# Two layers of graph convolution: layer one by relation ahead of the gathers, its messages summed by static ranges of destinations, layer two all dense

## The reference

```python
edge_index = jnp.stack([src, dst])
h = jnp.maximum(_layernorm(x, axis=-1), 0.0)
# layer one: x + _L0(h)
h_all = jnp.einsum('ni,roi->rno', node_repr, weight)
msgs = h_all[edge_types, src]
messages = jax.ops.segment_sum(msgs, dst, num_segments=node_repr.shape[0])
# + bias
h = jnp.maximum(_layernorm(x, axis=-1), 0.0)
# layer two: x + _L1(h)
h = x @ W
src, dst = edges and one loop per node; deg = segment_sum(1, dst)
norm = dinv[src] * dinv[dst]
out = segment_sum(norm[:, None] * h[src], dst) + b
return jax.nn.leaky_relu(out, negative_slope=0.2)
```

## Time and profile before

| | |
|---|---|
| median of three runs | 2851.63 us (2846.8 to 2854.67) |
| profiled execution, span | 2849.6 us |
| mean granted clock of TensorE | 0.928 |
| PE matmul busy | 2338.5 us, 82% |
| PE weight load busy | 1739.1 us, 61% |
| DVE busy | 1215.3 us, 43% |
| ACT busy | 1320.0 us, 46% |
| GpSimd (POOL) busy | 1693.0 us, 59% |
| moved by DMA | 464.38 MB, mean 163 GB/s |

### The profile page before, as it was taken

How to read it: one execution, slowest core, us unless ns; L and a number is a source line. 1 busy time by engine, 2 the same in 40 slices (tenths; PEclk the granted TensorE clock), 3 DMA queues, 4 the chain that set the end, 5 groups by cost and what they waited for, 6 DMA issues and landing times.

```text
span 2849.6 us, 45882 instructions
## 1 busy us (share of the span) xinstructions
PE 2338.5 (82%) x15616; PEld 1739.1 (61%) x15616; DVE 1215.3 (43%) x3492; ACT 1320.0 (46%) x3283; POOL 1693.0 (59%) x1754
## 2 busy tenths in 40 slices
PE   2357677777887888888888999999999999989887
PEld 2356666666666666666666666666666666656345
DVE  8345556556556565555555222222222222222228
ACT  5336655565656566565666343434344343433000
POOL 4666666656656666666666666666666666662530
PEclk9578888888999999999999999999999999999999
DMA  8335446545555655656556455545454454543665
GB/s 278 90 100 154 146 156 183 159 148 170 187 173 178 193 170 185 189 175 201 174 168 205 146 160 157 160 145 167 137 157 146 138 155 143 156 134 86 200 177 170
DMA packets 325692, 464.38 MB, mean 163 GB/s; under 512 B 61414, under 2 KB 252822, under 8 KB 325462
## 3 DMA queue, kind: packets, MB, share of 16 engines
q0 software_dynamic: 83168, 228.90, 28.3%
q1 hardware_dynamic: 198198, 149.60, 17.5%
q10 hardware_dynamic: 44096, 82.95, 7.8%
HBM read 352.28 MB, written 109.01 MB: 162 GB/s over the span
## 4 chain that ended last, share of the span: by engine, by line
PE 70%; issue 11%; ACT 7%; DVE 4%; another core or an unknown queue 3%; ACTq 1%; DMA 1%; POOL 1%; DVEq 0%; POOLq 0%; SPq 0%
PE ps_slot L1556 24%; PE ps_slot L1630 15%; PE ps_proj L1587 13%; PE ps_aux L1630 11%; PE ps_slot L1601 6%; ACT staging_f L1202 2%; ACT gap_f L1257 2%; ACT onehot_f L1265 1%; ACT acc_f L1188 1%; DVE hots_f L1435 1%; DVE acc_f L1478 1%; DVE acc_f L1483 1%; DVE acc_f L1475 1%; DVE hots_f L1432 1%
## 5 line engine op out<-in xcount | busy, mean ns | idle before, releaser
L1058 POOL DMA_INDIRECT rows_f<-table,idxT x1617 | 1565.3, 968 | 904.8 <-issue 404.4
L1556 PE MATMUL ps_slot<-onehot_f,rows_f 128*128 128x128 f32 x6468 | 916.1, 295 | 138.7 <-issue 71.9
L1556 PEld LDWEIGHTS ps_slot<-onehot_f,rows_f 128*128 128x128 f32 x6468 | 864.4, 207 | 188.8 <-issue 125.7
L1257 ACT ACTIVATE gap_f<-iota,keyT 128x128 bf16<-128x128 bf16 x1617 | 529.4, 394 | 91.8 <-issue 44.8
L1202 ACT ACTIVATE staging_f<-ps_slot 128x400 bf16<-128x400 f32 x768 | 348.0, 500 | 479.7 <-remote 228.7
L1265 ACT ACTIVATE onehot_f<-gap_f 128x384 f32<-128x384 bf16 x539 | 278.4, 516 | 560.2 <-remote 349.0
L1630 PE MATMUL ps_slot<-abuf_f,stash_f 128*128 128x512 bf16 x1890 | 457.6, 387 | 51.0 <-issue 48.8
L1432 DVE TENSOR_TENSOR hots_f<-iota_m_f,key_e_f 128x400 bf16<-128x400 bf16 x768 | 279.1, 363 | 455.2 <-PE ps_slot L1601 234.3
L1630 PE MATMUL ps_aux<-abuf_f,stash_f 128*128 128x512 bf16 x1710 | 410.9, 390 | 20.4 <-issue 19.5
L1587 PE MATMUL ps_proj<-w0t,acc_f 128*128 128x256 f32 x1600 | 389.7, 394 | 20.0 <-issue 19.2
L1346 DVE TENSOR_TENSOR acc_f<-ps_slot,acc_f 128x256 f32 (+1 forms) x561 | 232.0, 414 | 404.6 <-remote 220.8
(11 more groups left out here) (159 smaller groups left out, 816.4 us busy)
## 6 DMA issues: line engine op xcount, KB each, us to landing
abuf_f<-counts_d SPq DMA_DIRECT2D x120, 640.0 KB
rows_f<-table,idxT POOLq DMA_INDIRECT x1683
stash_f<-table SPq DMA_DIRECT2D x20, 960.0 KB
table<-hs_f SPq DMA_DIRECT2D x50, 192.0 KB
table<-xres SPq DMA_DIRECT2D x10, 640.0 KB, 7.6
x_d<-x_f SPq DMA_DIRECT2D x50, 128.0 KB
acc_f<-x_d SPq DMA_DIRECT2D x50, 128.0 KB, 2.2
xt_f<-in_x_dram SPq DMA_DIRECT2D x48, 128.0 KB
```

The lines of the kernel that those rows point to most:

```text
L1058: eng.indirect_dma_start(rows0[:, k, c, :], None, V["table0"], bass.IndirectOffsetOnAxis(ap=idxT[:, n * LOT + c:n * LOT + c + 1], axis=0)) ...
L1257: last = eng.activation(gap[:, n % 2, c, :], iota[:, :], ACT.Abs, scale=-1.0, bias=V["key"][:, n * LOT + c:n * LOT + c + 1])
L1556: last = eng.matmul(o[:, b * W:(b + 1) * W], rows0[:, k, c, b * P:(b + 1) * P], onehot[:, n % HOTS, c, :], start=(c == 0), stop=(c == LOT ...
```

## The change

Layer one is turned round: the first block projects every tile of nodes with all eight matrices and stores the results, and the gathers fetch messages that are ready.

- `table0` has 50 x 128 x 8 rows, one for each node and relation, each in three bf16 pieces of 256 (high, middle and low part of the float32 number): 1536 bytes a row. The index of an edge is (source + 64) x 8 + type.
- In the first block PE takes each tile through two transposes (`turn`), DVE copies them (`copy_turned`), and PE projects in two halves of four relations (`project`, `k = 2t + h`), each into two banks of PSUM; the halves alternate between two such pairs. ACT casts a half to bf16 (`high`), DVE subtracts (`remainder`), ACT casts the rest (`middle`), GpSimd subtracts again (`low`), and SP stores the tile, of which `parts` holds two. The preparation of the edges is spread among the tiles by number.
- In the second block a slot is a quad of four chunks. DVE builds a one-hot of 128 destinations (destination modulo 128) for each chunk. Destinations fall into 98 windows of 128 that step by 64; which chunks belong to which window is fixed at build time, and the first block checks that it is so. PE sums a window's chunks in one PSUM bank (three bf16 matmuls of 256 columns a chunk), and DVE adds it to the rows of x, in two or three parts.
- The bias is added on its own in stage A. The float32 sums, `acc`, its clearing, the projection in tiles and the bias in three pieces are gone.
- Layer two counts 800 windows (all 50 tiles) over `COUNT_SLOTS = 320` slots. The gathers behind the loop are gone. There are 13 groups (the last of two tiles) and 10 batches, so 260 pieces. The plan's account has `PACE = 3.9` and 3.6 us a piece. Two banks serve the closes instead of four, and six the late dense pieces instead of four.

The path for edges that don't fit (`aggregate_any`) is changed as well; it does not run here.

```diff
-RING0 = 7
+RING = 6
-PACE = 3.85
+PACE = 3.9
+PIECE = 3.6
+COUNT_SLOTS = 320
-    table0 = nc.dram_tensor("table0", (T * P, DF), f32).ap()
+    table0 = nc.dram_tensor("table0", (T * P * R, DF3), bf16).ap()
 # SP, first block
+                for t in range(T):
+                    eng.wait_ge(S["lo"], 2 * (t + 1))
+                    eng.dma_start(table0[t * P * R:(t + 1) * P * R, :].rearrange("(p r) d -> p (r d)", p=P),
+                                  parts[:, t % 2, :, :].rearrange("p r d -> p (r d)")).then_inc(s_t0[t % 2], 16)
 # ACT, first block
+                def high(k):
+                    t, h = divmod(k, 2)
+                    eng.wait_ge(S["pj"], k + 1)
+                    if t >= 2 and h == 0:
+                        eng.wait_ge(s_t0[t % 2], 16 * (t // 2))
+                    eng.activation(parts[:, t % 2, h * R // 2:(h + 1) * R // 2, 0:DF],
+                                   pair_bank(k).rearrange("p b (r d) -> p (b r) d", d=DF), ACT.Copy).then_inc(S["hi"], 1)
+                for t in range(T):
+                    high(2 * t)
+                    if t > 0:
+                        middle(2 * t - 1)
+                    if t + 2 < T:
+                        normalize(t + 2)
+                    high(2 * t + 1)
+                    middle(2 * t)
 # GpSimd, first block
+                def low(k):
+                    t, h = divmod(k, 2)
+                    eng.wait_ge(S["mid"], k + 1)
+                    rows = parts[:, t % 2, h * R // 2:(h + 1) * R // 2, :]
+                    eng.tensor_tensor(rows[:, :, 2 * DF:DF3], r1[:, k % 2, :, :], rows[:, :, DF:2 * DF], ALU.subtract).then_inc(S["lo"], 1)
 # PE, first block
+                    for h in range(2):
+                        k = 2 * t + h
+                        if k >= 2:
+                            eng.wait_ge(S["r1"], k - 1)
+                        for j in range(2):
+                            r = h * R // 2 + 2 * j
+                            for b in range(NB):
+                                last = eng.matmul(pair_bank(k)[:, j, :].rearrange("p (r d) -> p r d", d=DF), ht[:, t % 2, b, :], w0t[:, r:r + 2, b, :],
+                                                  start=(b == 0), stop=(b == NB - 1))
 # GpSimd, second block
-                for c in range(LOT):
-                    eng.indirect_dma_start(rows0[:, k, c, :], None, V["table0"],
+                if n >= RING:
+                    eng.wait_ge(s_pe, n - RING + 1)
+                for c in range(QUAD):
+                    eng.indirect_dma_start(rows[:, k, c, :], None, V["table0"],
 # DVE, second block
+                eng.tensor_tensor(onehot[:, n % HOTS, :, :], iota4[:, :, :],
+                                  V["key"][:, n * QUAD:(n + 1) * QUAD].unsqueeze(1).to_broadcast([P, P, QUAD]), ALU.is_equal).then_inc(s_oh, 1)
+                    add_rows(u, P // 4, P // 2, s)
+                    add_rows(u, P // 2, P, s)
+                    add_rows(u + 1, 0, P // 4, s)
 # PE, second block
+                for c in range(QUAD):
+                    i = n * QUAD + c
+                    s = PL.window[i]
+                    if PL.opens[i] and s >= 2:
+                        eng.wait_ge(s_msg, windows_added(s - 1))
+                    for p in range(3):
+                        last = eng.matmul(window_part(s), onehot[:, n % HOTS, :, c], rows[:, k, c, p * DF:(p + 1) * DF],
+                                          start=(PL.opens[i] and p == 0), stop=(PL.closes[i] and p == 2))
 # Plan
-                pe += 1.3 + 0.28 * len(self.win.get(n - LEAD, ())) + (3.45 if n >= LOTS and n % LOTS in PROJECT_AT else 0.0)
-            limit = (n + 1) * PACE + (3.0 if n < self.nlot else 0.0)
+                pe += 1.45 + 0.31 * len(self.win.get(n - LEAD, ()))
+            limit = (n + 1) * PACE + 3.0
```

More of the change, by code:

```diff
@@ L335, in _ @@
             @block.vector
             def _(eng):
-                seg_f, base, rel, orig = (small[:, i, :] for i in range(4))
                 ne = [0]
@@ L494, in _ @@
-                if ahead(n - 5):
-                    eng.wait_ge(S["acp"], n - 5)
-                eng.transpose(ps_slot[0:KT, n % 6, 0:P], small[:, 2, :], ident[:, :]).then_inc(S["etp"], 1)
-                n += 1
-                eng.wait_ge(S["below"], (KC + 1) // 2)
-                eng.wait_ge(S["below_odd"], KC // 2)
-                for b in range(D.looks):
-                    m = min(P, D.nall - b * P)
-                    for i in range(KC):
-                        last = eng.matmul(ps_proj[0:m, b:b + 1], below[:, i, b * P:b * P + m], one_w[:, :], start=(i == 0), stop=(i == KC - 1))
@@ new lines, in turn_edges, with first_chunks @@
+                def turn_edges(i):
+                    if i == 0:
+                        eng.wait_ge(S["edge"], 2)
+                    if i > 0:
+                        eng.wait_ge(S["acp"], i)
+                    a, k = divmod(i, KT)
+                    for q in range(LOT):
+                        last = eng.transpose(ps_aux[:, q * P:(q + 1) * P], ef[a][:, k, q * P:(q + 1) * P], ident[:, :])
+                    last.then_inc(S["etp"], 1)
+                def first_chunks():
+                    eng.wait_ge(S["below"], (KC + 1) // 2)
+                    eng.wait_ge(S["below_odd"], KC // 2)
+                    for b in range(D.sets):
+                        for i in range(KC):
+                            last = eng.matmul(ps_proj[:, b:b + 1], below[:, i, b * P:(b + 1) * P], one_w[:, :], start=(i == 0), stop=(i == KC - 1))
+                    last.then_inc(S["subp"], 1)
@@ L790, in __init__, with choose @@
             here += 1
-        self.slots = max(max(self.fin), self.work) + 3
-    def choose(self, D, n, todo, selfs, counted, stored):
-        ready = [u for u in todo if n >= max(counted[u[0]], stored[u[1]]) and (u[0] < EARLY_GROUPS or n >= counted[-1])]
-        if n >= self.tail:
-            ready += list(selfs)
+        self.slots = max(max(self.fin), self.work, self.whole[-1] + 4) + 3
+    def choose(self, n, todo, counted, stored):
+        ready = [u for u in todo if n >= max(counted[u[0]], stored[u[1]])]
         if not ready:
@@ L801, in choose @@
         now = self.stash[-1][0] if self.stash else 0
[L802 to L807 removed]
+        return min(ready, key=lambda u: (u[1] != now, u[1], u[0]))
 def both_layers(nc, D, V):
```

1176 lines of the change are left out of this document (456 added, 720 removed).

## The result

The changed kernel takes 3371.99 us (median of four runs, 3366.74 to 3379.76), the kernel before 2853.15; the ratio is 1.183, 95% interval 1.181 to 1.186. Foreseen were 3060 us, 2900 to 3200: the direction is right, the size lies outside the range.

What follows compares the result with a forecast made beforehand. PE was taken to bound the old loop, GpSimd's gathers the new one and the table's store the prologue. Prologue 558, loop 2110 and tail 394 sum to 3062, plus 2: say 3060 us, range 2900 to 3200.

Steps and rivals of the forecast that it cites:

- The prologue: Before the first gather: a ring of waits through the table's store costs 10.6 us a tile; 558 us, 483 lost.
- PE's pace: Rival, prologue: quicker stores leave PE's 7.35 us a tile, first gather at 409, whole 2915 us; chance 8%.
- The loop: First to last gather: the bound turns from PE to GpSimd, 2516 falls to 2110 us, 406 gained.
- PE's loop work is 403 x 1.45 + 800 x 0.31 + 153 x 3.3 = 1340 us, with room even at the clock of 0.91: Loop: quads' matmuls, counted windows and 153 dense pieces take PE 1340 us, so PE has room.
- All of these stand beside the next term: Loop: work of PE (1340 us), DVE (3.7 us a quad) and ACT is hidden beside GpSimd's 2110 us.
- GpSimd's own term: Loop: GpSimd's 1647 gathers, looks and fetches, at 1.25 to 1.30 us each, take 2110 us.
- a sign only for quads that come too fast: Loop: the forecast is wrong if quads come under 4.6 us.
- the three terms: Whole kernel: prologue 558, loop 2110 and tail 394 us, summed to 3062.
- DVE's masks: Loop: GpSimd's issue 4% longer beside DVE's masks (0.984 against 0.948 us); by the skill's rule at most 170 us added.
- The tail: Behind the last gather: 107 dense pieces with 50 closes between them, PE over 90% busy; 394 us against 258.
- Transfers as the bound: Rival, loop: rows from the 78.6 MB table cost 40 to 70% more, +120 to +380 us, put at 3250; chance 10%.
- The cheaper gather: Rival, loop: the 0.30 us ahead of each gather shrinks; at 0.95 each, loop 1640 and whole 2590 us; chance 14%.

Runs made afterwards that it cites:

- e4: Changed kernel with each tile of the table stored in two halves in the first block, on a second-kind chip: 2950.74 us.
- e10: Changed kernel with GpSimd gathering one chunk of a quad instead of four (403 gathers), PE multiplying as often, first-kind chip: 2246.91 us.
- e1: Changed kernel with gathers fetching only the first 512 of a row's 1536 bytes, PE multiplying them three times, second-kind chip: 3040.16 us.
- e2: Changed kernel with edge indices altered so that gathers read from the first 9.7 MB of the table, not 78.6, second-kind chip: 3036.60 us.
- the same two edited programs: Changed kernel with 512-byte gathers, and with counts' transfers cut: 3040.16 and 3037.03 us on the second kind, 3386.80 and 3359.93 on the first.
- e17: Changed kernel with GpSimd clearing a 128x128 tile after each gather and waiting for that, second-kind chip: 3377.36 us.
- e7: Changed kernel with half stores and PACE = 5.0 instead of 3.9, moving 57 dense pieces into the loop, first-kind chip: 3100.95 us, ratio 1.102.
- e8: Changed kernel with half stores, PACE = 5.0 and COUNT_SLOTS = 280 instead of 320, first-kind chip: 3059.42 us, one run.
- e12: Same edits as e8, timed again on a first-kind chip against the kernel before: 3092.24 us, ratio 1.083.
- e18: Changed kernel with PE multiplying each chunk's three pieces twice, gathers unchanged, second-kind chip: 3044.58 us.
- the three variants at 3037 to 3040 us: e1, e2 and e3, three edits of the changed kernel on a second-kind chip: 3040.16, 3036.60 and 3037.03 us.
- e3: Changed kernel with stores and loads of counts cut to 16 KB and less, second-kind chip: 3037.03 us.
- e11: Same edit as e3 (counts' stores and loads cut to 16 KB and less), on a first-kind chip: 3359.93 us.

## Why the prediction was right and wrong

- The prologue: right in its mechanism. The first gather came at 518.9, not 558, a tile takes 9.71 us ((509.4 - 33.6) / 49), not 10.6. Off were the store (5.1 us, foreseen 6.0), low (2.13, foreseen 1.9) and the hand-overs: the tile shown takes 9.38 us for 1.02 + 1.05 + 2.13 + 5.1 = 9.30, where 0.6 us were foreseen for the four. The store's 1.5 us of fixed cost were about right and its rate of 350 GB/s was not: with e4's half stores, 3.3 us for 786 KB, the two sizes give some 437 GB/s and 1.5 us, an estimate from medians to 0.1 us. Of its rival, PE's pace, e4 shows what it would have been: 433, at 8.0 us a tile and not 7.35. The Trainium skill (DMA: Bandwidth & Descriptors, Anatomy of one DMA) gives its fit, 2.0 us and bytes over 436e3, for transfers that GpSimd issues; this store is SP's. Applied to it all the same, it estimates 5.6 us and for the half ones 3.8. They landed in 5.1 and 3.3: the rate agrees, the fixed part is half a us less.
- The loop: the step that failed is "PE's loop work is 403 x 1.45 + 800 x 0.31 + 153 x 3.3 = 1340 us, with room even at the clock of 0.91", and with it "All of these stand beside the next term". The term that the sum put at nothing is PE's idle "issue". The work was sized within an eighth: 1178 us busy at a clock of 0.96 (e10), 1439 at 0.83 (e1). But of the 770 us of room (in e1 PE waits 698 us for rows), 696 went in the standstill, and its busy time rose by another 188 (1626 against e1's 1439). The clock, 0.77 for 0.83, accounts for some 110 of these by its ratio; the rest isn't settled. PE, in order and with a ring of six quads behind it, became late: GpSimd waited 348 us for buffers, and the loop is 339 longer. The standstill is what tips it: all else that PE does in the loop, 1626 + 82 + 54 = 1762 us, would have fitted into 2110. GpSimd's own term was right: 2110 / 1647 = 1.281 a gather foreseen, 2120.4 / 1647 = 1.287 in e1. A quad took 6.1 us; the prediction had named a sign only for quads that come too fast.
- The rows had it. The earlier trace rows give 71.9 and 121.9 us of "issue" ahead of PE's L1556 and L1601, at a time when PE was the late engine. I read the idle time as room. It was 270 us that PE lost without a cause shown, and a forecast that replaces a lot of three gathers every 4.67 us by GpSimd issuing without a pause had to ask what these 270 come with. Its size could not have been read from them: by the gather they give 0.17 us, and the changed kernel lost 0.43.
- The chip: on the second kind the three terms hold. e1, whose edit leaves the waits as they are, has 521, 2120 and 394 us, together 3036 where 3062 were summed: the prologue is 37 us shorter than foreseen and the loop 10 longer. Against that chip's kernel before, at 2435, it is 25% and not 7%: the base was read from one chip, and no rival allowed for another.
- DVE's masks: 2110 was reached with a slope of 4% for GpSimd beside DVE. The sentence of the Trainium skill (SBUF — State Buffer, SBUF: two separate sides), by which up to 170 us might have been added, isn't borne out in that size: e1's 2120 leaves room for 10. Whether the one-hots' instructions are in the mode that it speaks of, no run shows.
- The tail: right, 398.6 for 394, PE 98% busy.
- Transfers as the bound, a rival: fell by e2 (0.67 us a gather from either range; 0.70 foreseen).
- The cheaper gather, the rival on the other side: fell. The 0.30 stayed wherever one gather by index followed another without a wait.

What the standstill is, stays open. Shown is that it comes with gathers by index, that neither fewer bytes nor less other traffic takes it away, and that with the same two edited programs a chip of the second kind has none. Whether it depends on how close the gathers stand, or on their share of GpSimd's time, e17 was to tell and couldn't; nor does any run on the first kind vary what PE does beside the same gathers, other than by the dense pieces of e7, e8 and e12, though the kernel before, with little more than a third of it a gather, asks for that. It isn't a matter of more fetched instructions: queue 8, of kind "instruction", shows 109 packets and 1.79 MB on both kinds. That these are PE's is shown by e18, where PE's instructions alone were added and it moved 2.41 MB. The Trainium skill (Runtime: NRT & Kernel Launch, Instruction fetch mechanics) calls the cost of fetching the next block mostly hidden; no run here shows otherwise, and none resolves when a block arrives.

## What to carry to other kernels

Idle time behind "issue" on an engine that works in order is no room to fill: find what it comes with, and scale it by what the change does to that. (Work put beside it can still displace part of it, as in e7 and e8; it doesn't vanish.) When layers of buffers hide an engine's delay, add its own losses to its work before calling it hidden. And where a loop passes from one engine's pace to another's, a second chip can give another answer: here the change costs 18 to 19% on one kind of chip and, by the three variants at 3037 to 3040 us, some 25% on the other. On the second kind both kernels are quicker, the kernel before by some 400 us and the changed one by some 330.

## What the runs showed of the hardware that was not expected

- Chips of one type, each seen in one session, differ by 15 to 17% on the kernel before (2435 and 2443 against 2813 to 2854 us). In the profiled kernels the pace of gathers is the same on both (median 946 to 959 ns), and so is DMA's time for one (0.67 to 0.70 us of sixteen engines for 1536-byte rows, after, e2, e3 and e11).
- On chips of the first kind PE at times issues in steps of 0.70 us while GpSimd gathers by index: 1, 55, 304 and 522 to 604 such steps for 403, 806, 1209 and 1612 gathers in the changed kernel (the variants with more dense work aside), with 44, 128, 360 and 643 to 696 us of idle "issue"; 216 and 262 steps with 270 and 246 us in the kernel before, with 1617. On the second kind there are at most 3 steps, and no idle "issue" in the loop.
- GpSimd subtracts 128x1024 float32 less bf16 in 2.13 us (median; 2.23 on average), and issues a plain transfer in 0.54 us against 0.95 by index; 64 rows take 0.91.
- A store of 1.5 MB from SP's queue lands in 5.1 us and one of 768 KB in 3.3.
